# Splitting the gated FFN rows into high and low halves two tiles at a time

## The reference

```
ffn(v)  = (sigmoid(v q(w1)^T) * (v q(w2)^T)) q(w3)^T          hidden width 1408
attn(v): dt_raw, b, c = v W_x^T   (128 + 16 + 16 wide);  dt = softplus(dt_raw W_dt^T + b_dt)
         h_t = exp(-dt_t exp(A_log)) * h_(t-1) + dt_t * b_t * v_t    (512 channels x 16 states)
         y_t = sum over states of h_t * c_t  +  v_t * D
x = x + 0.5 ffn(layernorm(x));  x = x + attn(layernorm(x));  x = x + 0.5 ffn(layernorm(x))
```

## Time and profile before

| | |
|---|---|
| median of 3 runs (lowest to highest) | 790.04 us (789.42 to 791.45) |
| profiled execution: span from first to last instruction | 788.1 us |
| what lies around that span | not in the profile; the median is 1.9 us above the span |
| PE, DVE, POOL, ACT busy | 82%, 84%, 77%, 67% |
| mean granted PE clock | 0.94 |

### The profile page before, as it was taken

The page is one execution under the profiler, slowest core; times in us unless marked ns, Lnnn a source line. Parts: engine busy times, 40 slices in busy tenths (PEclk is TensorE's granted clock), DMA queues, the critical chain, the costliest instruction groups (busy, mean ns, idle before and its releaser), DMA issues.

```text
span 788.1 us, 13737 instructions
## 1 busy us (share of the span) xinstructions
PE 644.3 (82%) x4852; PEld 525.4 (67%) x4852; DVE 662.6 (84%) x1053; ACT 530.6 (67%) x1137; POOL 604.7 (77%) x479
## 2 busy tenths in 40 slices
PE   4697785579889988998899889988899887357878
PEld 3576663267668776886688767876787766245767
DVE  3872799689998999899989999899889987899721
ACT  5776665667686777766795779576867784556431
POOL 0081898589898998899889899799889978689512
PEclk9999998679999999999999999999999999578989
DMA  9500579668875897498668776788758875876000
GB/s 360 165 1 3 165 164 199 168 141 177 187 180 129 180 208 184 103 204 194 151 139 204 164 166 167 173 168 195 179 135 172 184 175 124 186 170 127 27 1 27
DMA packets 42437, 121.06 MB, mean 154 GB/s; under 512 B 5888, under 2 KB 14848, under 8 KB 42368
## 3 DMA queue, kind: packets, MB, share of 16 engines
q0 software_dynamic: 18864, 68.69, 45.9%
q1 hardware_dynamic: 23504, 51.49, 20.1%
HBM read 47.03 MB, written 4.46 MB: 65 GB/s over the span
## 4 chain that ended last, share of the span: by engine, by line
DVE 32%; PE 32%; issue 13%; ACT 13%; POOL 7%; DMA 2%; DVEq 1%; ACTq 0%; POOLq 0%
PE work L402 23%; DVE states L911 19%; PE stat L402 7%; DVE shared L922 7%; POOL hid_lo L1088 4%; ACT decay L727 3%; POOL shared L1104 2%; DMA shared<-shared 2%; DVE hid L881 2%; ACT L656 1%; PE decay L402 1%; ACT dt L715 1%; ACT q L745 1%; ACT L715 1%; ACT L659 1%
## 5 line engine op out<-in xcount | busy, mean ns | idle before, releaser
L402 PE MATMUL work<-x_hi,q 128*128 128x256 f16 x1408 | 328.0, 281 | 47.5 <-DVE hid L881 20.4
L1104 POOL TENSOR_TENSOR shared<-u,b_row 128x1024 f32<-128x1024 f32 x127 | 345.0, 2735 | 0.5
L402 PE MATMUL work<-x_lo,q 128*128 128x256 f16 x1408 | 326.9, 281 | 0.0
L911 DVE TENSOR_TENSOR_SCAN states<-decay,last_state,shared 128x256 f32<-128x256 f32 x448 | 303.7, 738 | 10.0 <-ACT decay L727 2.4
L727 ACT ACTIVATE decay<-dt,a_neg 128x256 f32<-128x256 f32 x512 | 220.2, 466 | 98.3 <-DVE states L911 97.5
L402 PEld LDWEIGHTS work<-x_hi,q 128*128 128x128 f16 x1408 | 142.3, 101 | 83.0 <-DVE hid L881 32.7
L1088 POOL TENSOR_TENSOR hid_lo<-hid,hid_hi 128x256 f16<-128x256 f32 x176 | 139.9, 1015 | 73.3 <-ACT hid_hi L690 73.1
L402 PE MATMUL work<-hid_hi,q 128*128 128x256 f16 x693 | 155.0, 274 | 14.8 <-POOL hid_lo L1088 7.8
L1117 POOL DMA_DIRECT2D shared<-shared x124 | 133.5, 1077 | 36.9 <-DVE shared L922 21.7
L922 DVE TENSOR_TENSOR shared<-states,c_row 128x1024 f32<-128x1024 f32 x128 | 155.5, 1215 | 5.8 <-issue 0.2
L402 PEld LDWEIGHTS work<-x_lo,q 128*128 128x128 f16 x1408 | 142.0, 101 | 21.8 <-issue 1.4
(11 more groups left out here) (102 smaller groups left out, 569.5 us busy)
## 6 DMA issues: line engine op xcount, KB each, us to landing
shared<-shared POOLq DMA_DIRECT2D x131, 512.0 KB, 6.2
b_row<-bc_dram SPq DMA_DIRECT2D x32, 512.0 KB, 5.1
c_row<-bc_dram SPq DMA_DIRECT2D x32, 512.0 KB, 5.2
x_in<-xT SPq DMA_DIRECT2D x8, 512.0 KB, 6.2
outT<-shared SPq DMA_DIRECT2D x7, 512.0 KB, 3.2
shared<-w1T SPq DMA_DIRECT2D x4, 704.0 KB, 7.3
shared<-w2T SPq DMA_DIRECT2D x4, 704.0 KB, 11.8
shared<-w3T SPq DMA_DIRECT2D x3, 768.0 KB, 13.5
```

Source lines behind the costliest of these rows:

```text
L402: return nc.tensor.matmul(out, lhsT, rhs, start=start, stop=stop)
L911: nc.vector.tensor_tensor_scan(out=states[:, k, :], data0=decay[pair][:, k % 2, :], data1=dbx[:, g % DBX_RING, k, :], initial=state, op0=A ...
L1104: nc.gpsimd.tensor_tensor(dbx[:, g % DBX_RING, :, :], u[:, par, :, :], bcast(b_row[:, group % 2, n % ROWS, :]), ALU.mult).then_inc(dbx_don ...
```

## The change

ACT's copy and POOL's subtraction are made once for two tiles. At an even h (but the last, h = 10) nothing is issued; at an odd h one instruction covers h - 1 and h, 128x512 in place of 128x256, and its semaphore counts up by 2. Tile 10 stays alone. The instruction stands where that of the odd tile stood. The tables, the waits of PE and DVE and the ring are as before; the wait for the pass before (`down_done`) goes from h = 0 to h = 1.

```
+        def split_of(which, h):
+            lo = h - 1 if h % 2 else h
+            slot = hid_slot(which, lo)
+            return h + 1 - lo, slice(lo, h + 1), slice(slot, slot + h + 1 - lo)
+
+        def closes_split(h):
+            return h % 2 == 1 or h == KH - 1
...
             def hidden_hi(f, which, h):
-                unit = KH * f + h
-                act.wait_ge(hid_done, unit + 1)
-                if h == 0 and not (isinstance(f, int) and f == 0):
+                if not closes_split(h):
+                    return
+                count, tiles, slots = split_of(which, h)
+                act.wait_ge(hid_done, KH * f + h + 1)
+                if h == 1 and not (isinstance(f, int) and f == 0):
                     act.wait_ge(down_done, 2 * f)
-                nc.scalar.activation(hid_hi[:, h, :], hid[:, hid_slot(which, h), :], ACT.Copy).then_inc(hi_done, 1)
+                nc.scalar.activation(hid_hi[:, tiles, :], hid[:, slots, :], ACT.Copy).then_inc(hi_done, count)
...
             def hidden_lo(f, which, h):
-                unit = KH * f + h
-                pool.wait_ge(hi_done, unit + 1)
-                nc.gpsimd.tensor_tensor(hid_lo[:, h, :], hid[:, hid_slot(which, h), :], hid_hi[:, h, :], ALU.subtract).then_inc(lo_done, 1)
+                if not closes_split(h):
+                    return
+                count, tiles, slots = split_of(which, h)
+                pool.wait_ge(hi_done, KH * f + h + 1)
+                nc.gpsimd.tensor_tensor(hid_lo[:, tiles, :], hid[:, slots, :], hid_hi[:, tiles, :], ALU.subtract).then_inc(lo_done, count)
```

## The result

The changed kernel takes 794.65 us (median of 5 executions, 794.31 to 797.39) against 790.04 us (789.42 to 792.06): ratio 1.0061, 95% interval 1.0041 to 1.0080, slower by 4.6 us. The forecast was 794.0. The profiled execution is the longest of the five: its span is 795.6 us, the other four have 792.5 to 792.9, and before had 788.1. In its code the same instructions stand some lines lower: the matmul helper is L411, the copy L701, the subtraction L1101, `hidden` L892, the residual L899.

What follows compares the result with a forecast made beforehand. No engine is free; the chain, shared by DVE and PE, passes through the FFN 2 down product waiting on POOL's tiles. Terms 2.2 + 0.4 + 0 + 1.0 + 0.45 = +4.0 us on 790.0 give 794.0 us, range 790.6 to 796.5.

Steps and rivals of the forecast that it cites:

- Steady chunks, 4 x 0.54: Chunks 1 to 4: POOL's pair (6,7) ends later, so PE's FFN 2 down product runs later; +2.2 us in all.
- The sentence that costs ACT at nothing: Before a steady chunk's down product: ACT's wide copies save 15.8 us busy time but change nothing, PE having its own work.
- Chunk 5, +0.4: Down product closing chunk 5: POOL's pair (6,7) ends later, PE reaches h = 10 at 575.1 instead of 574.69; +0.4 us.
- Chunk 6, 0: Chunk 6: DVE's `hidden` of h = 9 waits longer, but DVE later idles 4.11 us for PE; put at 0.
- Chunk 7, +1.0: Last chunk: pairs (4,5) and (6,7) each take 0.49 us longer, delaying PE's start and the mean; +1.0 us.
- First pass, +0.45: First pass: POOL's pairs and DVE's quantisation hold each other up, PE at 56.6 instead of 56.15; +0.45 us.
- POOL's price: POOL's subtraction of two tiles: 1.16 us alone, 1.12 us in a run, against 0.67 us for one tile.
- (a): Rival: shorter work on POOL counts, 10% less of its 31.5 us on the chain; 786.9 us, chance 6%.
- (b): Rival: slack absorbs the steady chunks' delay, only the first pass and chunk 7 remain; 791.4 us, chance 19%.
- (c): Rival: a 512-wide subtraction costs twice the 256-wide, 1.34 us, so all delays are larger; 797 us, chance 13%.

Runs made afterwards that it cites:

- e1: Changed kernel with pairs only in passes 3, 5, 7, 9, 11, single tiles in the others; 794.01 us, ratio 1.0048 to the kernel before.
- e8: Changed kernel with ACT copying single tiles again, POOL still subtracting in pairs; 794.73 us, ratio 1.0044 to the kernel before.
- e10: Changed kernel with ACT in single tiles, PE's first wait for tiles 0 to 5 and one more before h = 6; 793.64 us, ratio 1.0031.
- e13: Changed kernel with pairs (0, 1), (2, 3), (4, 5) only, then tiles 6 to 10 alone; 795.52 us, ratio 1.0064 to the kernel before.
- e3: Changed kernel with pairs (1, 2), (3, 4), (5, 6), (7, 8), tiles 0, 9, 10 alone, ring turned one slot; 785.22 us, ratio 0.9942.
- e6: Odd pairs as in e3, with PE's first wait for tiles 0 to 4 and a wait before each later h; 786.24 us, ratio 0.9919.
- e12: Odd pairs as in e3 in all passes but 3, 5, 7, 9, 11, which have single tiles; 785.39 us, ratio 0.9931 to the kernel before.
- e4: Changed kernel with PE's first wait for tiles 0 to 5 and one more wait before h = 6; 793.59 us, ratio 1.0049.

## Why the prediction was right

**The time.** 794.0 forecast, 794.65 measured. The terms, one by one:

*Steady chunks, 4 x 0.54.* Confirmed in size: a clean chunk is 0.51 us longer in e1 and 0.55 in e8. The mechanism was right but not alone. The prediction moved POOL and held everything else still; e8, which is that kernel, gives its +0.72 and +0.55 to the hundredth. In the changed kernel ACT's wide copy moves the square and the statistics by 0.2 us as well. The sentence that costs ACT at nothing, since PE "has its own work to the last", is the step that failed: that last work waits for ACT. It did not change the sum, because the two delays lie side by side and only the later one counts. What does count is when PE reaches h = 10: counted from PE's last up matmul before the statistics (before 406.96 - 402.77 = 4.19 us), it comes later by 0.52 us in e1's clean chunk, 0.54 in e8's, 0.40 in e10's, 0.34 in e13's and 0.04 earlier in e3's (chunk 2), and these chunks are 0.51, 0.55, 0.41 and 0.34 us longer and 0.05 shorter.

*Chunk 5, +0.4.* Confirmed in e1, where the chunk is 0.49 us longer with a stretch at half clock at the same place in both kernels. It follows the pattern of the others.

*Chunk 6, 0.* The predicted wait of `hidden` h = 9 is there, 1.18 us, and is given back only in part by shorter waits behind it (the residual's 4.11 is 3.94): the chunk is 84.48 us long against 84.10, each at a granted clock of 0.98. The term that was put at nothing is about 0.4 us in these two profiles. (The eight single tiles come to 0.67 + 7 x 0.62 = 5.0 us, not 5.06, which changes nothing.)

*Chunk 7, +1.0.* PE's idle time is 3.86 us where 2.89 + 1.0 was predicted, so the wait is right; that it costs the kernel 1.0 us is not shown. From chunk 7's first product with c to the end, before and after:

```profile
669.82:788.09 118.27, 82.06 (x606) 66.62 (x606) 77.75 (x114) 53.74 (x121) 64.97 (x52) 0.82 0.41 90
...
677.01:795.60 118.59, 79.74 (x606) 65.46 (x606) 77.77 (x114) 52.95 (x111) 63.12 (x41) 0.84 0.40 89
```

That is +0.3 us, and e1, with single tiles in pass 14, has 118.5. On the way the sum's mean is late by more: DVE waits 2.29 us for it in place of 0.65. PE's product behind the idle time takes 12.0 us in place of 11.0, at half clock for its first 5 us in place of 3. About 1.0 us came back in the last pass, from the mean to the end.

*First pass, +0.45.* PE's h = 10 at 56.61, predicted 56.6; the residual +0.47. The Trainium skill, "SBUF — State Buffer", Who interferes with whom, says that a DVE instruction with two SBUF inputs contends with a GpSimd instruction that reads SBUF, and that the shared ports are an exclusive lock. The trace agrees: 2.54 us for a pair that overlaps DVE's quantisation, 1.16 for one that does not.

*POOL's price.* 1.16 us for a pair that follows an idle stretch, as the one at 408.62, and 1.79 - 0.67 = 1.12 us from its start to the next one's: as taken. The mean of 1441 ns in the group holds the waits behind an earlier instruction (29 of the 80 take 1.15 or 1.16 us).

**The rivals.** (a) fell: 13.8 us less on POOL and none of it in the time. Of grouping, the Trainium skill, "Perfetto Trace Analysis", Optimizing Scalar/DVE Operations, says of ScalarE and VectorE that, where they are not saturated but cause bubbles on other engines, breaking up instructions may let work finish sooner. The trace agrees for GpSimd: e8's pairs have the bracket of 0.55 us ahead of PE's product, single tiles none. (b) fell with the clean chunks, (c) with the price.

**The sum.** In the profiles the terms come to 4 x 0.51 + 0.5 (chunk 5) + 0.4 (chunk 6) + 0.3 (chunk 7) + 0.5 (first pass) = 3.7 us, against 4.0. The steady chunks were worked out; that the sum is as near as it is owes something to luck, since chunk 7 was put 0.7 us too high and chunk 6 0.4 us too low, as far as profiles with stretches at half clock in those chunks can tell.

**What was missing** is the clock. It accounts for about 1.85 of the 2.34 us by which chunk 4 is longer in the profiled execution. The forecast's terms come to 4.0 of the median's 4.6 us without it; whether the median holds some of it is not shown. The other executions have a mean granted clock only, and that does not tell: 794.48 us and the profiled 797.39 both have 0.931.

## What stays open

Why a stretch at half clock falls into 22 of the 33 steady chunks with 2.3 to 2.4 us of idle PE and not into the others no run here separates, nor whether the shorter idle time is what keeps it out of e3, e6 and e12. In e12's profile the missing stretches are nearly all of what is won.

## What to carry to other kernels

Widening an instruction moves its first input's result to the time of its last; look which tile the consumer's first wait asks for, and let that tile close a group (odd pairs, e3); left alone behind three pairs (e13) it still cost 0.34 us a chunk. When a consumer starts without a gap, follow the work that fills it too: here it came from the same engine that was being widened. Removing one of several arrivals that lie close together wins little (e10) or nothing (e4); a wait then shows inside the product instead of ahead of it.

## What was not expected of the hardware

A stretch of PE at half clock can begin in the middle of a steady chunk, after idle times that the chunk has in the kernel before as well. PE in chunk 3 of the changed kernel:

```profile
395.00 0.70 PE L411 MATMUL stat<-square,mean_w 128*128 128x256 f32 x2 [0.93 <-ACT dt L726]
...
395.71 0.42 PE L411 MATMUL work<-x_lo,q 128*128 128x256 f16 x1
395.92 0.42 PE L411 MATMUL work<-x_hi,q 128*128 128x256 f16 x1
```

The step is 0.21 us where it is 0.109 at full clock, behind 0.93 us of idle PE. Before, chunk 3 has the same 0.93 us at this place and runs on at 0.109, so this idle time alone does not decide it. Such a stretch costs 0.80 us (chunk 3 before) to 1.46 us (chunk 5 before) of chunk. The times of one kernel spread over several us: the 28 runs of the kernel before in the last series go from 787.2 to 793.8 us. How much of that is the clock is not shown; 787.18 us has a mean granted clock of 0.935, 789.65 us one of 0.948.
